# Transformer block on one core: score maxima of batches 2 to 7 take the way by DRAM

## The reference

```
h = layernorm(x) * (1 + ca) + sa
q, k, v = split_heads(h @ wq + bq), ...          # 16 heads, 16 channels each
attn = softmax(q k^T / 4);  x = x + ga * ((attn v) @ wo + bo)
h = layernorm(x) * (1 + cb) + sb
shared = 2 experts on all tokens;  routed = 16 experts, gate = the 4 largest of softmax(h @ router^T), else 0
x = x + gb * (sum_e down_e(gelu(up_e h) * gate_e))      # 18 experts, 128 wide
```

## Time and profile before

| what | value |
|---|---|
| median of 3 runs | 886.01 us (885.74 to 889.5) |
| profiled execution, its own time | 884.7 us |
| its span in the profile | 882.9 us |
| PE busy | 832.7 us, 94% |
| ACT busy | 684.3 us, 78% |
| DVE busy | 605.4 us, 69% |
| POOL busy | 397.1 us, 45% |
| granted clock of PE, mean | 0.986 |
| bytes moved | 77.18 MB in 47,306 packets |

### The profile page before, as it was taken

How to read it: one execution, slowest core, us unless ns; L and a number is a source line. 1 busy time by engine, 2 the same in 40 slices (tenths; PEclk the granted TensorE clock), 3 DMA queues, 4 the chain that set the end, 5 groups by cost and what they waited for, 6 DMA issues and landing times.

```text
span 882.9 us, 19434 instructions
## 1 busy us (share of the span) xinstructions
PE 832.7 (94%) x7652; PEld 451.1 (51%) x7652; DVE 605.4 (69%) x1207; ACT 684.3 (78%) x1162; POOL 397.1 (45%) x351
## 2 busy tenths in 40 slices
PE   5778788999999999999999999999999999998998
PEld 3222333355545665566555555566555554555555
DVE  5665676786588866977688767886797758632452
ACT  4778688878988889888987899878987787855452
POOL 4455325225643364426623473426533353346472
PEclk9979799999999999999999999999999999999999
DMA  8006300533024512423024401530423300330140
GB/s 260 31 30 159 124 27 13 167 78 118 25 68 157 113 38 65 160 86 90 25 81 156 138 14 61 172 105 2 120 105 78 120 2 2 133 121 1 65 160 25
DMA packets 47306, 77.18 MB, mean 87 GB/s; under 512 B 6408, under 2 KB 41448, under 8 KB 43120
## 3 DMA queue, kind: packets, MB, share of 16 engines
q1 hardware_dynamic: 47216, 75.94, 27.3%
HBM read 63.47 MB, written 12.34 MB: 86 GB/s over the span
## 4 chain that ended last, share of the span: by engine, by line
PE 72%; ACT 12%; DVE 7%; issue 4%; POOL 4%; DMA 1%; SPq 0%; ACTq 0%; DVEq 0%
PE scalar_bank L1028 20%; PE down_bank L1193 18%; PE vector_bank L1101 8%; PE scalar_bank L1084 6%; PE vector_bank L1084 6%; PE vector_bank L1028 5%; ACT probs L787 3%; DVE neg_max L983 3%; PE scalar_bank L1113 3%; ACT q_aug L776 2%; PE vector_bank L1125 2%; ACT rows L759 1%; DVE gelu L970 1%; PE scalar_bank L1137 1%; ACT f_ring L742 1%
## 5 line engine op out<-in xcount | busy, mean ns | idle before, releaser
L983 DVE TENSOR_REDUCE neg_max<-vector_bank 128x1 f16<-128x512 f32 x487 | 309.2, 686 | 93.1 <-PE vector_bank L1084 88.2
L787 ACT ACTIVATE probs<-scalar_bank 128x512 f32<-128x512 f32 x484 | 262.5, 604 | 59.7 <-PE scalar_bank L1084 52.6
L720 POOL TENSOR_TENSOR act_lo<-gelu,act_hi 128x512 f16<-128x512 f32 x144 | 172.8, 1219 | 174.4 <-ACT act_hi L767 153.5
L1193 PE MATMUL down_bank<-down_hi,act_hi 64*128 64x256 f16 x1120 | 175.6, 271 | 0.5 <-PE down_bank L1193 0.2
L1193 PE MATMUL down_bank<-down_hi,act_lo 64*128 64x256 f16 x1120 | 174.6, 270 | 0.0
L1193 PE MATMUL down_bank<-down_lo,act_hi 64*128 64x256 f16 x1120 | 174.5, 269 | 0.0
L1084 PE MATMUL vector_bank<-k_aug,q_aug 64*128 64x512 f16 x487 | 131.1, 385 | 14.7 <-ACT q_aug L776 5.4
L970 DVE TENSOR_TENSOR gelu<-gelu,gates 128x512 f32<-128x512 f32 x128 | 110.1, 881 | 49.5 <-ACT gelu L824 49.4
L1084 PE MATMUL scalar_bank<-q_aug,k_aug 64*128 64x512 f16 x484 | 126.3, 384 | 4.1 <-ACT probs L787 1.9
L824 ACT ACTIVATE gelu<-scalar_bank 128x512 f32<-128x512 f32 x144 | 85.1, 596 | 57.2 <-PE scalar_bank L1028 38.6
L1101 PE MATMUL vector_bank<-probs,v_aug 128*32 128x512 f32 x960 | 111.9, 597 | 1.5 <-DVE z_lo L909 1.5
(11 more groups left out here) (202 smaller groups left out, 1258.1 us busy)
## 6 DMA issues: line engine op xcount, KB each, us to landing
gates<-gates_by_expert SPq DMA_DIRECT2D x32, 1024.0 KB, 5.1
q_aug<-q_parts SPq DMA_DIRECT2D x90, 64.0 KB, 2.8
k_aug<-k_parts SPq DMA_DIRECT2D x90, 64.0 KB, 2.6
x_pre<-in_x SPq DMA_DIRECT2D x8, 512.0 KB, 4.8
x_post<-in_x SPq DMA_DIRECT2D x8, 512.0 KB, 6.2
out<-x_post SPq DMA_DIRECT2D x16, 256.0 KB, 4.1
gates<-in_w_up SPq DMA_DIRECT2D x4, 576.0 KB, 10.7
gates<-in_w_down SPq DMA_DIRECT2D x4, 576.0 KB, 5.1
```

The source lines that it names most:

```text
L720: pool.tensor_tensor(act[1][:, c, :], gelu[:, n % NGELU, :], act[0][:, c, :], ALU.subtract).then_inc(s_elo, 1)
L787: scalar.activation(probs[:, n % U, :], src[:], ACT.Exp, scale=SCALE).then_inc(taken[kind], 1)
L983: dve.tensor_reduce(neg_max[:, (u // 2) % TT, at:at + 1], src[:], AX.X, ALU.max, negate=True).then_inc(done, 1)
L1193: ins = pe.matmul(o, act[a][at:at + 64, act_slot(b, c), tok:tok + P], wd[w][at:at + 64, c, :], start=n == 0 and k == 0, stop=c == NEX - 1 ...
```

## The change

For batches 2 to 7 (24 of the 32 groups) the turn has no part on PE, DVE or ACT. DVE writes the maxima into `max_columns`, 128 partitions x 2 x 4 heads x 4 tiles of 2 bytes. SP stores a group's columns to DRAM as rows (`maxima_by_row`, 4 heads x 512 values), waits for the store, and loads the rows by two transfers into rows 32 and 96 of `q_aug`. The first `exp` item of the group waits for these loads. There are two such buffers, one for odd and one for even groups. The `maxT` items no longer hold a PSUM bank. `e16` becomes the same memory as `shifted`.

The order changes as well: 8 of the 16 maxima of group g+2 are made in slot g, where most slots had 2 before; the turn stands right behind the last maxima of group g+1; and the tables of places are others throughout.

```diff
+def by_dma(kind, b):
+
+    return kind == "maxT" and b >= 2
 def lead(g):
 
+    if 8 <= g + 2 < NG:
+        return 8, 0, 0
     return LEAD["first" if g == FIRST else "light" if g + 1 < LIGHT else "full"]
...
-        for k, items in enumerate(maxima):
-            put(at["max"][8 - len(maxima) + k], *items)
-        put(at["turn"][0], *turn)
+        spots = (at["max"] + at["ahead"][:1])[-len(maxima + ahead):]
+        for k, items in enumerate((maxima + ahead)[:len(spots)]):
+            put(spots[k], *items)
+        ahead = ahead[len(spots) - len(maxima):]
+        put(spots[len(maxima) - 1] + .4 if maxima and by_dma("maxT", (g + 1) // G) else at["turn"][0], *turn)
...
-LEAD = {"light": (12, 0, 6), "full": (2, 0, 0), "first": (10, 4, 6)}
+LEAD = {"light": (12, 0, 0), "full": (10, 2, 0), "first": (12, 2, 6)}
...
+    max_d = nc.dram_tensor("maxima_by_row", (2, GH, TT, P), F16, kind="Internal").ap()
...
+        max_columns = sb("max_columns", [P, 2, GH, TT], F16)
...
-        e16 = sb("e16", [P, TT, NR])
+        e16 = shifted
...
+                elif by_dma(kind, b):
+                    wait(sp, taken["max"], PER["max"], b, U * (n + 1))
+                    sp.dma_start(max_d[n % 2].rearrange("j t p -> p j t"), max_columns[:, n % 2], allow_slow_non_contiguous=True).then_inc(s_maxout, 16)
+                    wait(sp, s_maxout, 16 * G, b - 2, 16 * (n + 1))
+                    for odd in range(2):
+                        sp.dma_start(qa[32 + 64 * odd:33 + 64 * odd, 2 * n:2 * n + 2, :].rearrange("o a s -> o (a s)"),
+                                     max_d[n % 2, 2 * odd:2 * odd + 2].rearrange("a t p -> (a t p)").unsqueeze(0)
+                                     ).then_inc(s_maxrow, 16)
...
-                elif kind == "maxT" and by_scalar(item):
+                elif kind == "maxT" and by_scalar(item) and not by_dma(kind, b):
...
-                    dve.tensor_reduce(neg_max[:, (u // 2) % TT, at:at + 1],
-                                      src[:], AX.X, ALU.max, negate=True).then_inc(done, 1)
+                    into = neg_max[:, (u // 2) % TT, at:at + 1]
+                    if by_dma("maxT", b):
+                        into = max_columns[:, n // U % 2, u % 2 * 2 + u // 8, (u // 2) % TT:(u // 2) % TT + 1]
+                        if u == 0:
+                            wait(dve, s_maxrow, 32 * G, b - 2, 32 * (n // U - 1))
+                    dve.tensor_reduce(into, src[:], AX.X, ALU.max, negate=True).then_inc(done, 1)
...
                     if kind == "exp" and n % U == 0:
-                        wait(pe, taken["maxT"], 4, b, n // U + 1)
+                        if by_dma("maxT", b):
+                            wait(pe, s_maxrow, 32 * G, b - 2, 32 * (n // U + 1))
+                        else:
+                            wait(pe, taken["maxT"], 4, b, n // U + 1)
...
+                elif by_dma(kind, b):
+                    pass
                 elif kind == "maxT":
                     wait(pe, taken["max"], PER["max"], b, U * (n + 1))
```

More of the change, by code:

```diff
@@ L110 @@
-SECOND = {"max": [1.04, 1.8, 5.06, 6.46, 7.23, 8.92, 11.32, 13.32], "exp": [0, 3.46, 5.06, 7.23, 9.55, 11.29, 12.99,
-    15.34], "down": [0, 3.0, 5.82, 9.36, 9.94], "up": [16.2, 17.32, 19.57, 22.09, 29.78], "gated": [18.12, 20.07,
-    24.4, 24.76, 28.65], "hi": [19.93, 20.39, 25.98, 27.96, 28.51], "turn": [16.37], "early": [5.38, 8.42, 16.4,
-    19.89, 21.24, 24.37, 24.8, 26.55], "pv": [14.02, 27.55, 29.9, 29.9], "ahead": [23.64, 24.79, 26.77, 29.85, 29.9,
-    29.9, 29.9, 29.9], "oraw": [29.9]}
@@ new lines @@
+SECOND = {"max": [0.9, 1.56, 4.43, 5.24, 6.46, 7.23, 8.92, 13.32], "exp": [0, 4.15, 5.06, 7.23, 9.55, 11.29, 12.99,
+    15.4], "down": [0, 3.0, 5.82, 9.36, 21.54], "up": [16.29, 17.55, 19.65, 22.09, 27.74], "gated": [18.62, 19.1,
+    20.07, 24.4, 28.65], "hi": [19.93, 21.06, 25.98, 26.07, 29.57], "turn": [23.55], "early": [3.35, 7.19, 12.24,
+    18.68, 19.6, 19.67, 21.63, 27.05], "pv": [13.55, 23.66, 28.16, 29.41], "ahead": [23.47, 24.62, 25.83, 26.6, 29.49,
+    29.73, 29.73, 29.9], "oraw": [29.9]}
@@ new lines @@
+THIRD = {"max": [0, 0, 4.59, 6.68, 8.18, 11.14, 13.36, 16.86], "exp": [2.04, 4.58, 5.25, 7.05, 9.05, 14.16, 14.67,
+    14.83], "down": [0.53, 5.21, 8.17, 12.23, 19.4], "up": [17.14, 17.26, 17.38, 20.16, 20.96], "gated": [0, 1.68,
+    21.16, 22.63, 26.87], "hi": [11.84, 19.85, 24.16, 24.32, 24.48], "turn": [29.42], "early": [6.77, 7.89, 16.71,
+    17.16, 19.5, 23.47, 23.75, 24.74], "pv": [21.71, 22.8, 24.34, 27.75], "ahead": [19.59, 20.78, 21.68, 21.86, 22.32,
+    29.41, 29.9, 29.9], "oraw": [29.9]}
@@ new lines @@
+LAST = {"max": [0, 2.27, 3.65, 5.47, 8.88, 10.42, 12.39, 13.56], "exp": [2.23, 3.37, 4.19, 7.06, 9.19, 12.26, 12.41,
+    13.86], "down": [0.1, 3.76, 5.64, 10.45, 12.32], "up": [16.34, 16.46, 20.53, 23.95, 24.25], "gated": [14.16, 27.5,
+    27.64, 29.2, 29.9], "hi": [17.27, 22.61, 23.39, 25.16, 26.11], "turn": [17.99], "early": [18.7, 20.19, 28.3, 29.9,
+    29.9, 29.9, 29.9, 29.9], "pv": [29.13, 29.13, 29.62, 29.84], "ahead": [28.04, 28.58, 28.74, 28.83, 29.36, 29.66,
+    29.66, 29.9], "oraw": [29.9]}
@@ new lines @@
+LIGHTLY = {"max": [10.49, 14.89, 17.16, 17.8, 18.31, 19.54, 25.8, 26.49], "exp": [0.55, 3.56, 6.05, 8.17, 10.79,
+    13.42, 14.45, 25.97], "down": [9.84, 20.06, 27.27, 29.49, 29.49], "up": [10.83, 16.63, 18.24, 19.1, 22.24],
+    "gated": [1.76, 2.07, 5.65, 6.95, 9.32], "hi": [0.56, 7.63, 8.4, 14.85, 19.89], "turn": [4.57], "early": [19.2,
+    20.46, 28.18, 29.9, 29.9, 29.9, 29.9, 29.9], "pv": [4.97, 22.14, 23.25, 26.58], "ahead": [4.7, 16.02, 20.65,
+    22.37, 23.85, 27.39, 27.39, 27.39], "oraw": [27.48]}
@@ new lines @@
+AFTER = {"max": [18.87, 20.56, 25.16, 25.2, 25.52, 26.51, 29.9, 29.9], "exp": [7.16, 8.65, 9.21, 11.41, 13.76, 13.86,
+    15.11, 17.46], "down": [0.64, 6.89, 12.89, 17.52, 25.7], "up": [0, 1.49, 10.08, 18.03, 22.34], "gated": [3.99,
+    16.74, 20.3, 29.9, 29.9], "hi": [11.81, 16.49, 22.81, 26.96, 27.17], "turn": [7.95], "early": [19.67, 22.06,
+    22.87, 23.59, 25.56, 27.27, 29.9, 29.9], "pv": [1.41, 29.14, 29.38, 29.9], "ahead": [0, 7.87, 8.89, 12.16, 14.29,
+    15.56, 15.74, 16.02], "oraw": [13.42]}
@@ new lines @@
+OPENING = {"max": [0.8, 1.64, 4.58, 9.4, 9.61, 10.41, 13.8, 18.96], "exp": [24.38, 24.87, 26.99, 27.35, 28.68, 28.68,
+    28.68, 28.68], "down": [1.11, 3.24, 12.44, 12.73, 17.86], "up": [11.74, 25.04, 26.99, 29.33, 29.73], "gated":
+    [3.87, 5.2, 9.02, 25.07, 26.13], "hi": [23.49, 24.62, 29.9, 29.9, 29.9], "turn": [20.95], "early": [17.49, 20.81,
+    22.54, 23.57, 24.23, 26.4, 27.01, 27.85], "pv": [1.51, 1.51, 1.83, 3.33], "ahead": [22.11, 26.46, 26.85, 28.29,
+    29.27, 29.86, 29.9, 29.9], "oraw": [29.9]}
@@ L292, in slot @@
     for k, items in enumerate(ahead):
-        put(at["ahead"][k], *items)
+        put(at["ahead"][0] + .1 * k, *items)
     if 0 <= g < NG:
@@ L335, in ring @@
             order.remove(banks)
-        if item[0] in kinds or values:
+        if item[0] in kinds and not by_dma(item[0], item[2]) or values:
             n = [n for n in order if n not in held][0]
@@ L974, in _ @@
                     dve.tensor_copy(o_raw[:, n, :], bank(("pv", n * TT, b))[:]).then_inc(taken["pv"], 1)
-                if kind not in V_KINDS or kind == "late" or by_scalar(item):
+                if kind not in V_KINDS or kind == "late" or by_scalar(item) or by_dma(kind, b):
                     continue
```

99 lines of the change are left out of this document (45 added, 54 removed), and 27 rows, old and new, of tables (BESIDE, MOVED).

## The result

The changed kernel takes 1070.14 us (median of 4 runs, 1060.71 to 1077.26) where the kernel before took 885.88 beside it: a ratio of 1.203, interval 1.198 to 1.208. One of the four runs (1077.26) fell in a slower state of the chip at a lower granted clock; the ratio and its interval are those of the others. The forecast was 878.1 us with a range of 867 to 894, so it missed by 192 us and on the wrong side. The profiled execution took 1067.84 us, its span is 1066.0.

A forecast was written before the change was run, and what follows sets the result against it. PE was taken to bound the kernel. 884.7 - 5.3 (removed turns) - 4.6 (new order) + 2.0 (wait at the last group) = 876.8; with 1.3 us to the runs' median, 878.1 us, range 867 to 894.

The forecast's parts named there:

- L: Time from the issue of SP's store of maxima to its landing in DRAM: taken as 4.5 us.
- The upper bound: Store's landing at the queue's mean packet time, 82 ns: 10.5 us, with a fixed part 11.8 us.
- The price I thought likely: Store's two-byte values at 8.6 ns a packet, from short runs at the start: 128 an engine, 1.1 us.
- The fixed part of 1.3 us: Part of the store's landing beside its packets, about 1.3 us, added to 1.1 us for 128 small packets an engine.
- The rival: Round trip of maxima through DRAM outlasts the PE work hiding it, if landing exceeds 10.1 us: 898 us, chance 0.11.
- cover: PE's work between a group's last maximum and first `exp`: 14.5 us group 3, 15.8 group 0, over 17 others.
- gates behind SP's wait: Expert gates queued on SP after group 3: DVE stands some 2 us a batch, priced at nothing behind `pv` items.
- SP's queue: Transfers queued on SP behind its wait for the store (gates, gb, next q, out rows) wait too; priced at nothing.
- What was removed: On PE, 24 turns of four transposes at 0.22 us each, in batches 2 to 7: 5.3 us saved.
- The copies: Turn copies removed, 28 us on ACT and 20 us on DVE: priced at nothing because PE's work hides them.
- The new places: Changed order of work in batches 2 to 7: 4.6 us of PE idle time regained, the least certain term.
- the places give nothing: Changed order regains no PE time; turns save 5.3 us, waits cost 2.0 and 2: 884.7 us, chance 0.23.

The follow-up runs named there:

- the idle store: Kernel before the change plus, each turn from batch 2, an unread 2-byte-value store of a constant that nobody awaits: 979.58 us on SP's queue, 997.77 on ACT's.
- the three forms I tried: Changed kernel, store wait and loads just before first `exp`: on SP, 1156.57 us; on POOL, 1202.14; on POOL with the store on ACT's queue, 1203.51.
- the control: Kernel before the change, PE transposes and copies kept, with one SP transfer placed behind its producer and one buffer sharing another's memory: 885.58 us, ratio 0.9995.
- whole runs at new places: Changed kernel, but maxima stored as they lie, 32 bytes a partition, and loaded as 2 KB, so rows are in wrong order: 886.5 us, ratio 0.999.

## Why the prediction was wrong

**The step that failed: L, the landing of the store.** I took 4.5 us, with bounds of 1.7 and 11.8. It is 16.5 from issue to issue of the loads (SP waits 16.0 of them). The upper bound was built from packets, 128 on an engine at the mean packet's 82 ns. The price I thought likely, 8.6 ns, was about right (9 ns by the queue's share above), and it did not help: a quarter of the packets landed hardly sooner. (The fixed part of 1.3 us stands there without its working; it fits the 1.3 us that SP waits for a store of whole runs.) What I left out was the other end of the transfer, where 32 writes of two bytes lie in 64 bytes of memory. The earlier trace rows was a load into SBUF, and I said so, but only moved L up by a little for it. A bound "from above" out of another kind of transfer was no bound.

**The rival was right in kind and too small.** It said: the trip outlasts its cover, from L = 10.1 on. With L = 16.5 the trip is 20.9 us against covers of 14.5, 15.8 and 17 twice: 6.4 + 5.1 + 3.9 + 3.9 = 19.3 us a batch; PE's waits for rows were 89.1 over the run, 14.9 a batch. So trip and cover were counted to about 1 us a group. The other 95 us the rival had not: the clock after each pause (7.9 us in the batch above, some 47 over six if they are alike), gates behind SP's wait (12.5 us of DVE where I had 2), and whatever the store holds up besides. The last two I can't tell apart. That the idle store alone cost 94 us, too, does not show that these are the same microseconds.

**SP's queue.** "While SP waits, what is queued behind it waits too" was right in kind, priced from the wrong L. The remedy that it suggests, to move the wait elsewhere, did not work in the three forms I tried. That transfers are held even when they are issued is shown (`out` in 17.8 us, the idle stores); how much of the loss is SP's queue alone stays open.

**What was removed** was priced rightly: 24 x 0.22 = 5.3 us, against 5.7 (3.6 to 7.8, from the ratio) with the turn on DVE at the old places, or 5.2 against the control. The copies, priced at nothing, are in the same figure and leave little for themselves. In the changed kernel ACT's busy time fell by 25.7 us (28 forecast); DVE's by 28.9 (20).

**The new places** were worth minus 8 us rather than plus 4.6. I had called this the least certain term and gave the rival "the places give nothing" 0.23; that they could cost was no case. The sign shows only where the trip is out of the way: whole runs at new places gave 886.5 where 881 would have been the sum of the other terms. Against the 184 us this error is small.

**The packets.** The Trainium skill, "DMA: Bandwidth & Descriptors", "Rules for kernel authors", has one descriptor for each element of a strided last dimension, and the trace agrees: the queue has 96,848 packets where it had 47,216, 49,632 more, of which 24 x 2048 = 49,152 are the values. I used that rule to count and stopped there; its advice to rearrange was the right one, and here it comes to whole runs of 32 or 64 bytes.

## What to carry to other kernels

A store of many short writes that lie side by side in DRAM is not priced by its packets: where a store turns rows and columns by its address pattern, look at what lies side by side in DRAM, and turn on an engine first, since a store of whole runs then holds SP for 1.5 us. Here another queue or a later wait did not hide the 2-byte store, and it made transfers on another queue land later; test such a store by an idle copy of it that nobody waits for. And where an unknown latency decides the sign, its upper end must come from a row of the same kind (a store to DRAM, of that width) or stay open.

## What the runs showed of the hardware that I had not expected

- 2048 writes of 2 bytes, 4 KB in all, land 16.5 us after their issue when 32 of them lie in 64 bytes of DRAM (changed kernel, mean of 24); 4.4 to 5.1 us when each has 64 bytes of its own; a quarter of them side by side still 14 to 16. With nothing else under way the DMA engines show as idle for much of the landing, a share of 0.00 from 464 to 472 us.
- Loads that pick 2048 single values show the DMA engines as busy instead, 55.0% of the span, and PE waits 10.9 us a group for them.
- Such a store slows other transfers: landings of 16.3 us at the median in place of 4.6 (tile x_post, idle store in the same queue), 10.2 in place of 4.1 (`out`, with the store in ACT's queue); and 94 us (ratio 1.109), or a ratio of 1.121 from ACT's queue, for 24 stores that nobody waited for.
- DVE turns 128x32 two-byte values in blocks of 32x32 in 0.20 us; SP's row for a small transfer with 8 runs is 0.635 us, and eight of them in a row hold SP for 5.4 us.
